# A graph network on one core: low one-hots of two groups in one comparison, and four instructions of the attention loop placed elsewhere

## The reference

```python
# layers 0 and 1: sums of neighbours' rows
summed = segment_sum(x[src], dst)          # layer 0, then mean, two products, batch norm, relu
agg = segment_sum(h[src], dst)             # layer 1, h = x / sqrt(out degree)
# layer 2: attention along edges; 8 heads of 16
q = x @ Wq; k = tensor_product(x[src'], edge_sh, wk, Cqk); v = the same with wv, Cv
attn = einsum('ehd,ehd->eh', q[target], k)
ex = exp(attn - segment_max(attn)[target]); alpha = ex / segment_sum(ex)[target]
upd = segment_sum(v * alpha) @ W_out
# layer 3: messages
messages = relu(concat(x[source], x[target]) @ W_msg + b_msg); agg = segment_sum(messages)
```

## Time and profile before

| | |
|---|---|
| median of 3 runs (lowest to highest) | 4864.38 us (4861.0 to 4865.03) |
| the profiled execution's own time | 4859.22 us |
| its span, first to last instruction | 4857.5 us |
| mean granted TensorE clock | 0.853 of full |
| busy, share of the span | PE 86%, DVE 79%, ACT 57%, POOL 47% |
| counting stage | VectorE busy 121.6 of 122 us |
| attention loop | PE busy 2466, DVE 2383 of 2600 us |

### The profile page before, as it was taken

How to read it: one execution, slowest core, us unless ns; L and a number is a source line. 1 busy time by engine, 2 the same in 40 slices (tenths; PEclk the granted TensorE clock), 3 DMA queues, 4 the chain that set the end, 5 groups by cost and what they waited for, 6 DMA issues and landing times. The chain is left out here.

```text
span 4857.5 us, 94822 instructions
## 1 busy us (share of the span) xinstructions
PE 4176.5 (86%) x21268; PEld 2878.9 (59%) x21268; DVE 3853.5 (79%) x9054; ACT 2780.1 (57%) x7136; POOL 2289.0 (47%) x2659
## 2 busy tenths in 40 slices
PE   3878877969999999999999999999996777777776
PEld 1322243546666666666666666666665666666665
DVE  8999956469999999999999999999993545545554
ACT  2777740048888888888888888888881000000000
POOL 1000000035555555555555555555540777777774
PEclk9999978879999999999999999999995555555555
DMA  3111116367887877877877877777760333333332
GB/s 85 80 80 80 80 53 246 148 155 170 173 173 170 174 171 169 174 171 170 174 171 171 174 170 172 173 170 173 171 146 21 80 76 76 76 75 78 76 77 48
DMA packets 576486, 639.86 MB, mean 132 GB/s; under 512 B 204473, under 2 KB 416249, under 8 KB 572483
## 3 DMA queue, kind: packets, MB, share of 16 engines
q1 hardware_dynamic: 517362, 554.10, 48.4%
q0 software_dynamic: 52288, 81.11, 8.0%
q10 hardware_dynamic: 6736, 3.53, 0.3%
HBM read 584.50 MB, written 53.94 MB: 131 GB/s over the span
## 5 line engine op out<-in xcount | busy, mean ns | idle before, releaser
L1332 POOL DMA_INDIRECT attn_rows<-x_twice,attn_idx x808 | 886.7, 1097 | 357.2 <-issue 242.8
L1719 POOL DMA_INDIRECT msg_rows<-a_rows,msg_idx x808 | 781.6, 967 | 363.7 <-issue 220.3
L1359 POOL TENSOR_TENSOR acc_den<-acc_den,attn_sums 128x256 f32 x808 | 553.4, 685 | 387.6 <-DVE attn_z_lo L1577 225.7
L1758 PE MATMUL msg_at_dst<-msg_bwin,msg_pick 128*128 128x64 f32 x1616 | 397.6, 428 | 271.2 <-DVE msg_pick L1784 249.7
L1697 ACT ACTIVATE msg_msg<-msg_pre 128x256 f32<-128x256 f32 x202 | 84.1, 417 | 943.6 <-DVE msg_pre L1798 943.6
L1758 PEld LDWEIGHTS msg_at_dst<-msg_bwin,msg_pick 128*128 128x128 f32 x1616 | 359.8, 328 | 351.6 <-DVE msg_pick L1784 325.3
L1572 DVE TENSOR_TENSOR attn_z<-attn_xt,attn_sh 128x512 f32<-128x512 f32 x808 | 540.4, 690 | 30.0 <-ACT attn_xt L1247 13.0
L1577 DVE TENSOR_TENSOR attn_z_lo<-attn_z,attn_z_hi 128x512 fp32r<-128x512 f32 x808 | 560.3, 693 | 0.2
L1270 ACT CAST attn_z_hi<-attn_z 128x512 fp32r<-128x512 f32 x808 | 496.7, 620 | 82.7 <-DVE attn_z L1572 76.1
L481 DVE TENSOR_SCALAR count_key_hot<-key_iota,key_tab 128x400 bf16<-128x400 f16 x1395 | 496.4, 356 | 0.0
L1361 POOL MEMSET acc_den<- 128x6656 f32 x1 | 5.6, 5645 | 963.9 <-POOLq L93 963.9
(11 more groups left out here) (288 smaller groups left out, 10660.1 us busy)
## 6 DMA issues: line engine op xcount, KB each, us to landing
attn_sh<-in_edge_sh SPq DMA_DIRECT2D x404, 640.0 KB, 8.1
attn_qwin<-q_rows SPq DMA_DIRECT2D x808, 64.0 KB
counts<-chunk SPq DMA_DIRECT2D x15, 3100.0 KB, 9.7
chunk_late<-counts SPq DMA_DIRECT2D x15, 3100.0 KB, 10.5
attn_dst<-dst_near SPq DMA_DIRECT2D x202, 128.0 KB, 3.1
attn_feat<-in_edge_feat SPq DMA_DIRECT2D x404, 64.0 KB
attn_mask<-dst_step SPq DMA_DIRECT2D x202, 128.0 KB, 2.9
msg_dst<-dst_near SPq DMA_DIRECT2D x202, 128.0 KB, 2.9
```

The lines of the kernel that those rows point to most:

```text
L1332: pool.indirect_dma_start(rows[p][:, t, :], None, dram["x_twice"], bass.IndirectOffsetOnAxis(ap=idx[p][:, t:t + 1], axis=0)).then_inc(rows ...
L1359: pool.tensor_tensor(window, window, sums[p][:, :, t, :], ALU.add).then_inc(added, 1)
L1719: pool.indirect_dma_start(rows[p][:, t, :], None, dram["a_rows"], bass.IndirectOffsetOnAxis(ap=idx[p][:, t:t + 1], axis=0)).then_inc(rows_ ...
L1758: mm = nc.tensor.matmul(at_dst[p][:, t * D:(t + 1) * D], pick[p][:, t, :], bwin[p][:, t, :], start=True, stop=True)
```

## The change

Four edits. In the counting stage the six comparisons that make `lo_hot` for the three slots of two groups become one comparison of 768 elements, before the first group's keys: `lo_iota` holds each number six times in a row, `lo_tab` is now fp16 and holds a group's three values side by side, and the second operand is a row of six values read again for each of the 128 numbers. So the columns of one slot's matrix now stand six elements apart in memory, and TensorE loads its weights with that step. The ring of `lo_hot` is three pairs. In the attention loop ScalarE's `empty_den` comes behind the first high part, not the second; VectorE's `make_pick` comes before the last product and last low part, not behind `vw`; GpSimd's `fade` is merged into `add`, ahead of its additions, and the fourth addition waits for the end of the round's scans, which `fade` had waited for.

```diff
         @block.vector    (count_and_sum)
+        PAIRS = 3
+        lo_hot = [ph.sb(f"lo_hot{r}", [P, P, 2 * SLOTS], BF16) for r in range(PAIRS)]
             def one_hots(g):
                 if g >= RING:
                     dve.wait_ge(counted, g - RING + 1)
+                if g % 2 == 0:
+                    if g >= 2 * PAIRS:
+                        dve.wait_ge(counted, g - 2 * PAIRS + 2)
+                    both = sb["lo_tab"][:, g:g + 2, :].rearrange("p g s -> p (g s)")
+                    nc.vector.tensor_tensor(lo_hot[g // 2 % PAIRS][:], sb["lo_iota"][:],
+                                            both.unsqueeze(1).to_broadcast([P, P, 2 * SLOTS]), ALU.is_equal)
                 for s in range(SLOTS):
-                    nc.vector.tensor_scalar(lo_hot[g % RING][:, s, :], sb["lo_iota"][:], sb["lo_tab"][:, s, g:g + 1],
-                                            None, ALU.is_equal)
                     ts = nc.vector.tensor_scalar(key_hot[g % RING][:, s, :], sb["key_iota"][:],
...
-                    mm = nc.tensor.matmul(bank[g % 4][:, 0:KEYS], lo_hot[g % RING][:, s, :], key_hot[g % RING][:, s, :],
+                    mm = nc.tensor.matmul(bank[g % 4][:, 0:KEYS], lo_hot[g // 2 % PAIRS][:, :, g % 2 * SLOTS + s], key_hot[g % RING][:, s, :],
...
         ScalarE's body (attention_loop)
                     high(g + 1, q, 0)
-                    high(g + 1, q, 1)
                 if not (is_first(g, 0) or is_first(g, 1)):
                     empty_den(p)
                 if next:
+                    high(g + 1, q, 1)
                     high(g + 1, q, 2)
...
         GpSimd's add
+                pool.wait_ge(low_ready, (KC - 1) * (min(g + 4, G) if isinstance(g, int) else g + 4))
                 if not is_first(g, 0):
                     pool.wait_ge(added, STEPS * g)
+                first_col = sb["acc_den"][:, :, bass.ds(bases[0], 1)]
                 pool.tensor_tensor(first_col, first_col, factor, ALU.mult).then_inc(added, 1)
                 for t in range(TG):
                     pool.wait_ge(added, STEPS * g + t + 1)
+                    if t == TG - 1:
+                        pool.wait_ge(topped, min(g + 3, G) if isinstance(g, int) else g + 3)
...
             with pool.Fori(0, G // 2 - 4) as n:
                 add(2 * n + 1, 1)
-                fade(2 * n + 2, 0)
                 gather(2 * n + 7, n + 3, 1, False)
                 add(2 * n + 2, 0)
-                fade(2 * n + 3, 1)
                 gather(2 * n + 8, n + 4, 0, False)
...
         VectorE's body
                 if next:
+                    split_most(*after(g, n, p))
+                if has_two(g):
+                    make_pick(*in_two(g, n, p))
+                if next:
                     split_end(*after(g, n, p))
...
-                if has_two(g):
-                    make_pick(*in_two(g, n, p))
                 if front:
                     maxima(g, n, p)
```

More of the change, by code:

```diff
@@ L232, in _ @@
             for s in range(SLOTS):
-                nc.scalar.copy(sb["lo_tab"][:, s, :], lo_ps[s][:].rearrange("p k g -> p (k g)")).then_inc(copied, 1)
+                nc.scalar.copy(sb["lo_tab"][:, :, s], lo_ps[s][:].rearrange("p k g -> p (k g)")).then_inc(copied, 1)
             act.wait_ge(padded, 64)
@@ L243, in _ @@
                       allow_small_or_imprecise_dtypes=True).then_inc(ranged, 1)
-            pool.iota(sb["lo_iota"][:], [[1, P]], base=0, channel_multiplier=0,
+            pool.iota(sb["lo_iota"][:], [[1, P], [0, 2 * SLOTS]], base=0, channel_multiplier=0,
                       allow_small_or_imprecise_dtypes=True).then_inc(ranged, 1)
@@ L465, in count_and_sum @@
         key_hot = [ph.sb(f"key_hot{r}", [P, SLOTS, KEYS], BF16) for r in range(RING)]
-        lo_hot = [ph.sb(f"lo_hot{r}", [P, SLOTS, P], BF16) for r in range(RING)]
+        PAIRS = 3
+        lo_hot = [ph.sb(f"lo_hot{r}", [P, P, 2 * SLOTS], BF16) for r in range(PAIRS)]
         tally = ph.sb("tally", [P, HB, CHUNKS])
@@ L1334, in gather, with add @@
                         bass.IndirectOffsetOnAxis(ap=idx[p][:, t:t + 1], axis=0)).then_inc(rows_in[p], 16)
[L1336 to L1340, removed]
+            def add(g, p):
+                bases = window_bases(nc, mybir.EngineType.Pool, sb, TG * g)
                 factor = ex[p][:, GE:GE + 1].unsqueeze(1).to_broadcast([P, 2, 1])
                 pool.wait_ge(ex_sb, g + 1)
-                pool.wait_ge(topped, min(g + 2, G) if isinstance(g, int) else g + 2)
+                pool.wait_ge(sum_sb, COPIES * (g + 1))
+                pool.wait_ge(low_ready, (KC - 1) * (min(g + 4, G) if isinstance(g, int) else g + 4))
                 if not is_first(g, 0):
@@ L1368, in _ @@
             gather(4, 2, 0, False)
-            fade(0, 0)
             gather(5, 2, 1, False)
             add(0, 0)
-            fade(1, 1)
             gather(6, 3, 0, False)
@@ L1375, in _ @@
                 add(2 * n + 1, 1)
-                fade(2 * n + 2, 0)
                 gather(2 * n + 7, n + 3, 1, False)
                 add(2 * n + 2, 0)
-                fade(2 * n + 3, 1)
                 gather(2 * n + 8, n + 4, 0, False)
             add(G - 7, 1)
-            fade(G - 6, 0)
             gather(G - 1, G // 2 - 1, 1, False)
-            for g in range(G - 6, G - 1):
+            for g in range(G - 6, G):
                 add(g, g % 2)
-                fade(g + 1, (g + 1) % 2)
-            add(G - 1, 1)
         @block.sync
@@ L1582, in split_begin, with split_most @@
                 make(*group, 1)
-            def split_end(*group):
+            def split_most(*group):
                 for c in range(KC - 3):
@@ L1588, in split_end @@
                 low(*group, KC - 3)
+            def split_end(*group):
                 make_last(*group)
@@ L1642, in first @@
                 split_begin(g, n, p)
+                split_most(g, n, p)
                 split_end(g, n, p)
@@ L1895, in program @@
                 counting_table("key_iota", [P, KEYS], FP16)
-                counting_table("lo_iota", [P, P], FP16)
+                counting_table("lo_iota", [P, P, 2 * SLOTS], FP16)
                 counting_table("key_tab", [P, SLOTS, GK * P])
-                counting_table("lo_tab", [P, SLOTS, GK * P])
+                counting_table("lo_tab", [P, GK * P, SLOTS], FP16)
                 setup(nc, dram, sb)
```

5 lines of the change are left out of this document (removed).

## The result

The changed kernel takes 4749.07 us (median of 4 runs, 4747.34 to 4750.78) beside 4862.69 for the kernel before (4 runs, 4860.78 to 4865.03): a ratio of 0.9761, 95% interval 0.9749 to 0.9773, or 113.6 us less. Its profiled execution took 4750.78 us, 108.4 less than the one of before, at the same mean clock of 0.853.

A forecast was written before the change was run, and what follows sets the result against it. VectorE was taken to bound counting, and a chain through several engines the attention round. Counting -106 and attention +6 made -100 us: 4759 from the profiled 4859.2, 4764 with the runs' median 5 us higher; range 4738 to 4815.

The forecast's parts named there:

- the likeliest case: Whole kernel: outcome as forecast, likeliest 4764 us, its own range 4742 to 4788, chance 0.68.
- The comparison: Counting, VectorE: one 768-element comparison costs 0.50 us, replacing six that cost 0.975 us per pair of groups.
- Counting in sum: Counting stage: 0.2375 us a group over 465 groups, 110 us, less 4 for ScalarE in the second chunk: 106 less.
- The weights: Counting, TensorE: weights six elements apart load near 99 ns, and even 187 ns stays hidden under 1.04 us a group.
- The rival of slow weights: Counting, TensorE: strided loads at 0.40 us add 124 us, giving 4994; chance 0.03, plus 0.05 for loads between 0.21 and 0.29.
- The denominators' copies: Attention, ScalarE: earlier copies remove TensorE's 0.45 us and VectorE's 0.375 us waits a round, alone worth up to 75 us.
- The pick: Attention, VectorE: moved ahead of `u`, it costs 0.50 us and changes the round by +0.03, 202 rounds by +6 us.
- GpSimd: Attention: `fade` ahead of the additions puts them some 0.45 us later, level with VectorE's next product; costed at nothing.
- the sum's 4759.2: Whole kernel: -106 + 6 = -100 us against the profiled execution's 4859.2, giving 4759.
- the unpacked comparison: Counting, VectorE: rival that the comparison runs one element a step, costs 0.88 us and gives 4848; chance 0.09.
- attention slower: Attention: rival with the pick at 0.65 us and a late fourth addition, +0.23 a round, +46 us, 4804; chance 0.11.
- attention faster: Attention: rival with a shorter chain through `u`, the round falling by all of 0.37 us, 4683; chance 0.04.

The follow-up runs named there:

- c_f32: Changed kernel with the comparison's number table `lo_iota` in 32 bits instead of 16: 5139.6 us, ratio 0.9942 to the kernel before.
- c_contig: Changed kernel with low one-hots laid out slot by slot, six rows of 128, each second-operand value repeated 128 times: 4843.4 us, ratio 0.9933 to the kernel before.
- lag: Changed kernel with VectorE's counting additions begun four groups later: ratio 0.9768 to the kernel before, counting 477.8 us.
- pick_lag: Changed kernel with the pick back behind `vw` and counting additions four groups later: 4697.24 us, ratio 0.9644 to the kernel before.
- pick_back: Changed kernel with only the pick put back behind `vw`: 4999.23 us on a slower chip, ratio 0.9702 to the kernel before.
- act_only: Changed kernel with pick and GpSimd's order put back, leaving the comparison's edit and ScalarE's move: 5009.53 us, ratio 0.9688 to the kernel before.
- pick_twice: Changed kernel with the pick's comparison made twice ahead of `u`, first into a spare buffer: 4817.7 us, ratio 0.9875 to the kernel before.
- pool_back: Changed kernel with only GpSimd's `fade` and `add` order put back: 5044.33 us on a slower chip, ratio 0.9766 to the kernel before.
- act_lag: Changed kernel with pick and GpSimd's order put back and counting additions four groups later: 4699.54 us, ratio 0.9636 to the kernel before.

## Why the prediction was right

The forecast was 4764 us, and 4749 came out: 15 us lower, inside the likeliest case's own range. The mechanism held too: the gain is all counting's, and in attention a wait for the copies was exchanged for one for `u`. Step by step:

- **The comparison.** Taken at 0.50 us between bounds of 0.475 and 0.88; it cost 0.469, the lower bound to 0.01. The argument, that half the width doubles the rate, was confirmed by c_f32 and is incomplete: c_contig has the width and not the rate. What a repeated value costs was not considered; that the layout chosen avoids it was luck as far as the argument goes. The second operand, a row of six read again, needed no allowance.
- **Counting in sum.** A pair gained 0.975 - 0.469 = 0.506 us, 465 groups 117.7. Measured were 110.7, so 7 are lost. I had taken 4 off, for ScalarE in the second chunk. The size is near by luck, the place is wrong: in that chunk VectorE is busy 29.00 of 29 us, and a group takes 0.934 us in both of the first two chunks (over 30 groups each). The loss is a wait for TensorE's applied sums at each chunk's start, and lag gave 5.6 of the 7 back. VectorE's idle time in the stage went from 0.8 to 7.4 us. It now passes a chunk faster, and TensorE's last application no longer comes before the first addition.
- **The weights.** Forecast near 99 ns, hidden up to 187; measured 125, hidden. The rival of slow weights falls.
- **The denominators' copies.** As forecast, both waits went. Their worth of up to 75 us if nothing else moved is a bound that one execution came near, the fastest of pick_lag, with 73.5 us less attention than before. pick_back's trace has 39 us less than before, and act_only, with ScalarE's edit alone, 26.
- **The pick.** The step held, with errors that offset each other. The product's latency is 1.26 us (1.22 forecast), the pick costs 0.44 (0.50), and the distance before was 1.725 (1.69). So -0.06 + 0.04 - 0.035 is -0.055 a round, 11 us, off the forecast +6: -5. Measured -0.4; the next products start later (0.21 us behind the last column's score in place of 0.18), which would be the rest. But traces of the same loop differ by up to 19 us, so agreement to a few us is luck, and what is shown is that the edits nearly cancel. pick_twice and pick_back show the pick's cost on the path from both sides: 0.35 us a round longer for 0.40 more ahead of `u`, 0.20 shorter for 0.44 less.
- **GpSimd.** Costed at nothing; the ratios of pool_back and of the pair of pick_lag and act_lag agree, within their intervals.

The miss of 15 us in the median is 8.4 in the profile (4750.8 against the sum's 4759.2): counting came out 4.7 lower and attention 6.4, the other stretches 2.7 longer. The other 7 are the profiled execution's place among the runs, 5 us under the median that I had then and 1.7 over it now. The rivals: the unpacked comparison would have needed 0.95 us; attention slower needed a pick of 0.65 us, and it cost 0.44; attention faster is what the kernel could have had in part with the pick left in place.

## What to carry to other kernels

When a wait is removed from a round, look at what the same edit puts on the path that takes over: here 0.45 us a round of waiting for copies became 0.37 us of waiting for `u`, since a comparison of 0.44 us had been moved out of the shadow of a product (1.26 us) to a place ahead of it. Work that nobody needs soon belongs into such a latency, and the two best versions both have that one move undone. And merging small instructions pays in full with 16-bit operands only if both step from one element to its neighbour: put the short repeated pattern innermost, not the repeated value, even if the consumer must then read with a step: of 111 us the other order left 24. Last, before a difference between two traces is explained, look at how far two traces of the same code lie apart: 0.2 us in the counting stage here, 19 to 34 in attention.

## What was unexpected of the hardware

- Weights whose columns stand six 16-bit elements apart load in 125 ns in place of 98, and the matmuls in front of which they load start 0.169 us apart either way.
- A 768-element comparison costs the same 0.869 us whether one operand is 32 bits wide or merely repeats a value: the rate has two levels here, 1.04 ns an element more or less exactly halved (0.400 us for 768 elements).
- The message loop took some 285 us longer on two of the chips (1316 to 1332 us against 1028 to 1034) with nothing in the kernel changed, and there alone attention has waits called remote. So a ratio between kernels of different groups is good to some 0.2 points only.
- The seven runs of pick_lag spread by 1% (4663 to 4711 us), while on the same chip the nine of the kernel before spread by 0.3% and the five of act_lag by 0.3%. Its fastest execution has TensorE idle for 0.06 us a round; why the others are slower no trace shows.
